# First keys and queries of the second attention in front of the last output tiles of the first, and an output bias made one product of stacked halves

## The reference, cut to what matters

```python
xn = _layernorm(x)                                   # x: 1024 x 512
s = _L0_attn_ref(xn, ...)                            # 8 heads of 8; out @ Wo_w.T + Wo_b
g = _silu(_L0_ffn_ref(xn, ...))                      # base product and 8 low-rank experts, top 2
x = x + s * g                                        # called x1 below
xn = _layernorm(x)
# second attention: 32 query heads, 8 key/value heads of 128
q = _rmsnorm((xn @ Wq.T)...); k = _rmsnorm((xn @ Wk.T)...); v = xn @ Wv.T
attn = softmax(q k / sqrt(128) + alibi, causal); s = (attn v) @ Wo.T
g = _silu(_L1_ffn_ref(xn, ...))                      # weights in 4-bit codes, two low-rank terms
x = x + s * g
```

## Time and profile before

| | us |
|---|---|
| median of three runs (lowest to highest) | 1482.02 (1481.35 to 1490.38) |
| profiled execution, its own time | 1485.61 |
| its span | 1483.8 |
| PE busy, share of the span | 1392.6 (94%) |
| DVE busy | 985.2 (66%) |
| ACT busy | 855.7 (58%) |
| POOL busy | 633.9 (43%) |
| the tail, from its first transposes (219.48) to the first matmul of slot 0 (280.16) | 60.7 |

### The profile page before, as it was taken

The page is one execution under the profiler, slowest core; times in us unless marked ns, Lnnn a source line. Parts: engine busy times, 40 slices in busy tenths (PEclk is TensorE's granted clock), DMA queues, the critical chain, the costliest instruction groups (busy, mean ns, idle before and its releaser), DMA issues.

```text
span 1483.8 us, 21377 instructions
## 1 busy us (share of the span) xinstructions
PE 1392.6 (94%) x7358; PEld 1087.5 (73%) x7358; DVE 985.2 (66%) x1851; ACT 855.7 (58%) x2103; POOL 633.9 (43%) x966
## 2 busy tenths in 40 slices
PE   4989988799999999999999999999999999989997
PEld 3733336588778888878887788888778887768786
DVE  6666644476787777777776777776786777775233
ACT  3345572465766666666766666666766666563211
POOL 4322353444454435545443445444554445433311
PEclk9989996899999999999999999999999999999999
DMA  4100021010020101011010201110020111023010
GB/s 139 64 1 1 1 94 59 15 30 30 29 73 2 58 20 54 21 39 59 15 41 19 73 20 39 42 31 30 30 72 1 44 34 38 28 66 133 15 58 28
DMA packets 35883, 61.02 MB, mean 41 GB/s; under 512 B 9056, under 2 KB 13280, under 8 KB 35776
## 3 DMA queue, kind: packets, MB, share of 16 engines
q1 hardware_dynamic: 35776, 59.66, 12.6%
HBM read 49.68 MB, written 9.96 MB: 40 GB/s over the span
## 4 chain that ended last, share of the span: by engine, by line
PE 66%; DVE 8%; issue 6%; ACT 2%; POOL 1%; DMA 0%; POOLq 0%; DVEq 0%; SPq 0%
PE T L2239 7%; PE T L1870 7%; PE T L1872 6%; PE T L1871 6%; PE S L1872 4%; PE S L1871 4%; PE S L1870 4%; PE WB L1870 4%; PE WB L1871 4%; PE WB L1872 4%; PE VB L1872 4%; PE VB L1870 4%; PE VB L1871 4%; PE T L2132 2%; DVE R L1648 2%
## 5 line engine op out<-in xcount | busy, mean ns | idle before, releaser
L848 POOL TENSOR_TENSOR RI<-SM,C 128x1 f32<-128x1 f32 x256 | 143.1, 559 | 503.7 <-ACT PB L1184 502.7
L1641 DVE CUSTOM_DVE_ANT_0 PB<-S,REL,SLC 128x128 f32<-128x128 f32 (+7 forms) x256 | 204.4, 813 | 82.3 <-PE S L1872 80.8
L1184 ACT ACTIVATE PB<-PB,NM 128x128 f32<-128x128 f32 (+7 forms) x256 | 198.9, 777 | 69.6 <-DVE NM L1641 63.5
L1249 ACT ACTIVATE R<-T 128x512 fp32r<-128x512 f32 x288 | 170.8, 594 | 100.7 <-PE T L2239 98.8
L849 POOL TENSOR_SCALAR PB<-PB,RI 128x128 f32<-128x128 f32 (+7 forms) x256 | 215.0, 840 | 25.2
L1648 DVE TENSOR_TENSOR R<-T,R 128x512 fp32r<-128x512 f32 x288 | 197.4, 688 | 42.3 <-ACT R L1249 23.8
L2239 PE MATMUL T<-C,PB 128*128 128x128 f32 x1152 | 176.6, 276 | 12.3 <-DVE R L1648 7.1
L2239 PEld LDWEIGHTS T<-C,PB 128*128 128x128 f32 x1152 | 134.1, 140 | 48.4 <-DVE R L1648 18.5
L1163 ACT ACTIVATE JUNK<-WB 128x128 bf16<-128x128 f32 x256 | 67.4, 278 | 95.2 <-PE WB L1872 95.2
L1870 PE MATMUL WB<-R,XT 128*128 128x512 f32 x288 | 117.5, 408 | 2.7 <-ACT G L1141 2.7
L1871 PE MATMUL WB<-R,XT 128*128 128x512 f32 x288 | 114.2, 397 | 0.0
(11 more groups left out here) (275 smaller groups left out, 3512.7 us busy)
## 6 DMA issues: line engine op xcount, KB each, us to landing
RAW<-w SPq DMA_DIRECT2D x86, 256.0 KB, 2.8
DQ<-codes SPq DMA_DIRECT2D x16, 352.0 KB, 3.5
DQ<-absmax SPq DMA_DIRECT2D x16, 352.0 KB, 3.0
dequantised<-DQ SPq DMA_DIRECT2D x16, 352.0 KB, 2.2
PB<-x SPq DMA_DIRECT2D x12, 256.0 KB, 3.3
PB<-dequantised SPq DMA_DIRECT2D x5, 512.0 KB, 4.4
PB<-x_scratch SPq DMA_DIRECT2D x8, 256.0 KB, 3.5
out<-PB SPq DMA_DIRECT2D x8, 256.0 KB, 2.0
```

The costliest lines, as they stand in the source:

```text
L848: ch.link(e.tensor_tensor(RI[:, k:k + 1], SM[:, k:k + 1], C[:, C_EXP + 5:C_EXP + 6], ALU.pow))
L1184: e.activation(pb(m, a, 0, L), pb(m, a, 0, L), ACT.Exp, scale=-1.0, bias=NM[:, k:k + 1], accum_out=SM[:, k:k + 1]).then_inc(exp_done, 1)
L1249: e.activation(r(PT + AT[i, ("PV", kb)] % 3 * 1024, 512), T[AT[known, it] % 2][:, :], ACT.Copy).then_inc(t_act, 1)
L1641: e.tensor_tensor_reduce(out=pb(m, a, 0, L), in0=bank[:, 0:L], in1=REL[:, TOK - L:TOK], scale=SLC[:, a:a + 1], scalar=3.0e38, op0=ALU.add, ...
```

## The change

It has three parts.

1. The tail has another order. KV 0, PQ 0 and KV 1 stand at its head, before or between the first OS and OH; KV 2, KV 3, SQ 0 and QT 0 follow in steps 1 and 2. PQ 1 now stands behind KV 6 and in front of KT 5, KT 6 and KV 7. The scores of the first query tile (new kind S0) are items of the tail and stand in front of QT 1. Keys in work lie in four buffers instead of two. `WB` goes WO 3, PQ 0, WO 4 instead of WO 3, WO 4.
2. The second, third and fourth of PQ's chunks of weights must be there earlier: their halves are made in units 27 to 31, and SP loads the last two behind the first store of x1 instead of behind four.
3. The bias product of `output0` has 64 rows of type fp32r instead of one row of float32. ACT copies the bias row on 64 partitions and makes 64 rows of 1/32 (behind the fourth of the QK products at the start of the kernel); DVE turns rows 32 to 63 into the low half in front of the first OS. The halves of O move from `OT + 512` to `PT + 1024`.

```diff
-W_AT = {("F", t): t for t in range(NT)}
+EARLY = 4
+W_AT = {}
+for _x in ([("F", t) for t in range(NT)] + [("WO", t) for t in range(EARLY)] + [("PQ", 0)] + [("WO", t) for t in range(EARLY, NT)] + [("PQ", 1)]):
+    W_AT[_x] = len(W_AT)
...
-HIGH_AT = {22: ("K", 0, 0), 23: ("K", 0, 1), 28: ("Q", 0, 0), 29: ("Q", 0, 1)}
-LOW_AT = {24: ("K", 0, 0), 25: ("K", 0, 1), 29: ("Q", 0, 0), 30: ("Q", 0, 1)}
+HIGH_AT = {22: ("K", 0, 0), 23: ("K", 0, 1), 26: ("Q", 0, 0), 27: ("Q", 0, 1), 29: ("Q", 0, 2), 30: ("Q", 0, 3)}
+LOW_AT = {24: ("K", 0, 0), 25: ("K", 0, 1), 27: ("Q", 0, 0), 28: ("Q", 0, 1), 30: ("Q", 0, 2), 31: ("Q", 0, 3)}
...
-KV_STEP = (1, 2, 3, 4, 6, 7, 8, 9)
+KV_STEP = (0, 0, 1, 2, 6, 7, 8, 10)
...
-    seq = [("XT", EARLY - 1)] if k == 0 else []
+    seq = [("XT", EARLY - 1), ("KV", 0), ("PQ", 0)] if k == 0 else []
     seq += token_items(EARLY + k, EARLY, NT)
...
+    if k == 9:
+        seq.append(("PQ", 1))
...
+    return seq + {1: [("SQ", 0)], 2: [("QT", 0)], 11: [("S0", 0), ("QT", 1)]}.get(k, [])
...
-        KN = [QN[:, 4 * HD:5 * HD], K2F[:, 3072:3200]]
+        KN = [QN[:, 4 * HD:5 * HD]] + [K2F[:, 3072 + k * P:3200 + k * P] for k in range(3)]
...
-            for t in range(EARLY):
-                store_x1(t)
+            store_x1(0)
             w1_first("Q", 0, 2)
             w1_first("Q", 0, 3)
+            for t in range(1, EARLY):
+                store_x1(t)
...
             qk(3, *QK_THEN[0])
+            act.wait_ge(in_rows, 16)
+            e.activation(r(PT + 2048, D, 64), ROWS[0:64, R_BO:R_BO + D], ACT.Copy).then_inc(bo_high, 1)
+            e.activation(r(PT + 2560, P, 64), IDENT[0:64, :], ACT.Copy, scale=0.0, bias=1.0 / 32).then_inc(ones_set, 1)
...
                     elif it[0] == "OS":
+                        if it[1] == 0:
+                            dve.wait_ge(bo_high, 1)
+                            e.tensor_tensor(R[32:64, PT + 2048:PT + 2560], ROWS[32:64, R_BO:R_BO + D],
+                                            R[32:64, PT + 2048:PT + 2560].bitcast(F32), ALU.subtract).then_inc(bo_low, 1)
...
-                e.matmul(WB[:, :], ONES, ROWS[0:1, R_BO:R_BO + D], start=True, stop=False)
+                e.matmul(WB[:, :], r(PT + 2560, P, 64), r(PT + 2048, D, 64), start=True, stop=False)
```

More of the change, by code:

```diff
@@ L260 @@
 T_LN0, T_OUT = 0, 24
-TAIL_HIGH = {0: ("Q", 0, 2), 1: ("Q", 0, 3)}
-TAIL_LOW = {1: ("Q", 0, 2), 2: ("Q", 0, 3)}
-KV_STEP = (1, 2, 3, 4, 6, 7, 8, 9)
-SC_STEP = (2, 3, 4, 5, 7, 8, 9, 10)
-KT_STEP = (3, 4, 5, 6, 8, 9, 10, 11)
-PQ_STEP, SQ_STEP, QT_STEP = (5, 9), (6, 10), (7, 11)
+KV_STEP = (0, 0, 1, 2, 6, 7, 8, 10)
+SC_STEP = (1, 1, 2, 3, 7, 8, 9, 11)
+KT_STEP = (2, 3, 4, 5, 8, 9, 10, 11)
 TAIL_STEPS = 12
 def tail_items(k):
-    seq = [("XT", EARLY - 1)] if k == 0 else []
+    seq = [("XT", EARLY - 1), ("KV", 0), ("PQ", 0)] if k == 0 else []
     seq += token_items(EARLY + k, EARLY, NT)
[L277 to L280, removed]
+    if k == 9:
+        seq.append(("PQ", 1))
+    seq += [("SC", b) for b in range(NT) if SC_STEP[b] == k]
+    if k == 11:
+        seq.append(("SQ", 1))
+    seq += [("KT", b) for b in range(NT) if KT_STEP[b] == k]
+    seq += [("KV", b) for b in range(1, NT) if KV_STEP[b] == k]
+    return seq + {1: [("SQ", 0)], 2: [("QT", 0)], 11: [("S0", 0), ("QT", 1)]}.get(k, [])
 TAIL = [x for k in range(TAIL_STEPS) for x in tail_items(k)]
@@ L543, in program @@
         ones_set = sem("ones_set")
+        bo_high = sem("bo_high")
+        bo_low = sem("bo_low")
         x1_ready = sem("x1_ready")
@@ L937, in add_x @@
             def add_x(t):
-                hold(pool, w_free, W_OUT + t + 1, p_passed)
+                hold(pool, w_free, W_AT["WO", t] + 1, p_passed)
                 hold(pool, in_x[t % 4], 16 * (t // 4 + 3), p_passed)
@@ L1127, in high_on @@
                 if t >= 2:
-                    act.wait_ge(w_full, W_OUT + t - 1)
-                e.activation(r(OT + 512 + t % 2 * 256, P), T[k % 2][:, 0:P], ACT.Copy).then_inc(high, 1)
+                    act.wait_ge(w_full, W_AT["WO", t - 2] + 1)
+                e.activation(r(PT + 1024 + t % 2 * 256, P), T[k % 2][:, 0:P], ACT.Copy).then_inc(high, 1)
             for x in range(NBX):
@@ L1209, in _ @@
                         high_q(b, T_AT[x] + 1, T[T_AT[x] % 2])
[L1210 to L1216, removed]
+                    elif kind == "S0":
+                        for a in range(4):
+                            exp1(0, a, P, a + 1)
+                    if x == ("KV", NT - 1):
+                        w1_high("K", 1, 0)
+                        w1_high("K", 1, 1)
             def lines(g, i, part):
@@ L1699, in _ @@
                     low_q(t, T_AT[x] + 1, T[T_AT[x] % 2])
-            for k in range(4):
-                dve.wait_ge(out_x1[k], 32)
-            dve.wait_ge(out_dq, 16)
+                elif kind == "S0":
+                    for k in range(4):
+                        dve.wait_ge(out_x1[k], 32)
+                    dve.wait_ge(out_dq, 16)
+                    for a in range(4):
+                        bias_max(0, a, P, S_PRO + a + 1, S[a % 2])
             dve.wait_ge(t_free, T_BASE)
             dve.sem_inc(v_split, NT)
-            for a in range(4):
-                bias_max(0, a, P, S_PRO + a + 1, S[a % 2])
             def combine(g, i, part):
@@ L2157, in _ @@
                 if kind == "PQ":
-                    project_q(block_of(b), W_PRO + b, lambda kt: C_PRO["Q", 0, kt])
+                    project_q(block_of(b), W_AT[x], lambda kt: C_PRO["Q", 0, kt])
                 elif kind == "WO":
                     output0(b, t_free, T_AT["OH", b] + 1)
+                elif kind == "S0":
+                    for a in range(4):
+                        if a < 2:
+                            pe.wait_ge(st_exp, 2 * NBX)
+                        scores1(0, a, P, a - 1 if a >= 2 else None, max(T_AT["KT", 0], T_AT["QT", 0]) + 1, S[a % 2])
                 elif kind in ("OS", "OH", "XT", "KV", "KT", "QT"):
                     k = T_AT[x]
-                    if kind in ("OS", "OH", "XT"):
+                    if kind in ("OS", "OH", "XT") or k < T_OUT + 2:
                         ring0(k)
@@ L2184, in _ @@
                         transpose_q(k, T[k % 2])
[L2185 to L2188, removed]
             def values1(g, i, kb):
```

39 lines of the change are left out of this document (16 added, 23 removed).

## The result

The changed kernel takes 1472.37 us (median of 8 executions, 1470.38 to 1474.42) against 1482.74 of the kernel before (8 executions, 1480.76 to 1490.38). The ratio on record is 0.9912, with a 95% interval of 0.9887 to 0.9937; it is estimated over all executions and is not the quotient of the two medians, which is 0.9930 and lies in the interval. By the medians that is 10.4 us or 0.7% less: within 1% of before, as forecast, and 4.1 us above the predicted 1468.3. The profiled execution took 1472.16 us, its span is 1470.4.

The account below looks back on a forecast made before the run. Bound: the last four tiles' chain from WO to XT at a low clock, and the idle end. Terms -2.2 - 5.4 - 2.3 - 4.0 + 0.2 = -13.7 us: 1485.6 to 1471.9, less 3.6: 1468.3 us; range 1460 to 1477.

Parts of the forecast that it names:

- 3.6 us: Median of the runs taken as 3.6 us below the profiled execution, so 1471.9 became 1468.3.
- The milestones: Signs behind XT 3: WO 4 ending near 13 us, XT 4 starting near 24, XT 7 ending near 35.
- The head of the tail: Start of the tail: 6.8 us of dense matmuls, so no fall of the clock 4.4 us behind XT 3.
- XT 3 to XT 4: Tail stretch: XT 4 starts at 24.0 us instead of 29.4, with a low clock between 16 and 23: -5.4 us.
- the two terms behind it: XT 4 to the end of XT 7, -2.3 us, and XT 7 to slot 0's score heads, -4.0 us.
- The bias product: The new product of 64 rows of fp32r takes 0.3 us instead of 1.05.
- The units: Units 24 to 31: four shorter products win 3.0 us, the wait for PQ's first chunk costs 0.8: -2.2 us.
- The copies: ACT's copies and DVE's subtraction for the bias, costing 0.2 us (0 to 1.0).
- XT 4 to XT 7: Stretch to the end of XT 7: 13.45 us before, now 11.2 at half clock: -2.3 us.
- the end: XT 7 to slot 0's first score heads: 23.0 us before, now 19.0: -4.0 us.
- Full clock: Rival: the clock stays full throughout the passage, sum -20.2 us, time 1461.8 us; chance 0.17.
- The dear product: Rival: the new bias product costs as much as the old, 5 us less gain, 1473.3 us; chance 0.07.

Follow-up runs that it names:

- order_only: The changed kernel with the bias product put back to one float32 row, without its two copies and subtraction: 1486.02 us, ratio 1.0003.
- bias_only: The kernel before with the third part of the change alone (bias product of 64 rows of fp32r): 1472.00 us, ratio 0.9923.
- float_64_rows: The kernel before with its float32 bias product given 64 rows instead of one: 1475.89 us, ratio 0.9951.
- fp32r_1_row: The kernel before with the new fp32r bias product cut to its first row, low half left out: 1473.05 us, ratio 0.9932.
- combined: Changed kernel, first keys' low halves before tile 7's gate, next ones after the last key's scaling, bias copies behind the router's exponential: 1471.86 us.
- after_again: The changed kernel run once more, nothing changed: 1473.55 us, ratio 0.9929 against the kernel before.
- filled: The changed kernel with 49 further matmuls that nothing reads, in front of the waits of the tail: 1468.07 us, ratio 0.9894.

## Why the prediction was right, and where it was not

**The number.** 1472.4 lies in the range, at the upper edge of the forecast's own (1464 to 1472). The sum of -13.7 answers to the profiles' -13.4, the medians' difference is 10.4. I took 3.6 us from the profiled execution as if it were a constant. It was an execution of before with a low mean clock (0.977; its executions near the median have 0.979), and the change removes low stretches, so part of the 3.6 was counted twice. The profiled execution of the changed kernel lies only 0.2 us below its median.

**The milestones** came as written or near it: WO 4's end 12.8 (12.9), XT 4 23.4 (24.0), XT 7's end 33.9 (35.2), the heads 53.8 (54 to 55), the fall of the clock 18.5 (some 15).

**The step that failed is the cause given for the clock.** "The head of the tail is now 6.8 us of dense matmuls, so I expect no fall at 4.4." The head is enough for that (order_only has it, the float32 rows, and no fall before 13.2), but it isn't needed: bias_only has no such head and no fall either. And it doesn't last: in order_only the clock falls right behind the first float32 row of the tail, and XT 4 comes at 28.8. What brings XT 4 forward is the bias product, either by its rows at an unchanged duration (float_64_rows, 7.1 us) or by its short type with one row (fp32r_1_row, 10.0). The prediction priced the product at its duration, 0.75 us each at full clock, and gave XT 3 to XT 4's 5.4 us and the two terms behind it to the order. The runs leave the order with nearly nothing (above). That the sum came out is partly luck: the order was priced too high and the product too low, and both were in the change.

**The bias product** costs 0.44 us to the next start, not 0.3. **The units** gave 1.3, not 2.2. 4 x 0.61 is 2.4; the wait for PQ's first chunk held the exponential 1.3 us, as counted (1.4), and costs 1.0 by combined, where it is gone, for my 0.8. It was the gate of tile 7 on POOL, ahead of the low halves, that made the load late.

**The copies** were put at 0.2 us. The start and units 0 to 23 lose 1.7: the first transposes of the shifts come 0.6 us later (79.57 for 78.98), which goes away in combined, and the clock is low for 20.5 us of the units instead of 17.0. after_again had 23.9, so no run ties this length to the copies.

**From XT 3 to XT 4** the working of the new order was right at full clock too (22.7 counted, 23.5 measured in filled). Its comparison was wrong: at full clock the old order takes 18.5, so the queries in front cost 5.0 us here, which the later terms return. The rows for LA were read the wrong way round: the one of 1.21 us begins 0.35 us behind the start of an addition (213.31 and 212.96 in the earlier trace rows), not ahead of it. In the changed kernel the LA of tile 4 took 0.88 us beside an addition, for the 1.0 counted.

**XT 4 to XT 7** at half clock (counted 11.2 to the end of XT 7, measured 10.5) and **the end** (19.0 counted, 20.0 measured) were right but for the scaling of the last key: 1.28 us beside POOL, 0.29 without. The Trainium skill (SBUF — State Buffer, "SBUF: two separate sides") says that DVE and GpSimd share a pair of ports as a lock, which the one that starts first holds for its whole instruction. The trace agrees: POOL starts 0.06 us ahead, and the scaling ends at 265.88, 0.1 us behind the first of POOL's two low halves (1.25 us each from 264.54).

**The rivals.** Full clock was priced at 1461.8; filled has it in the whole tail and takes 1468.1. Its three terms of the tail measured -5.9, -5.4 and -5.4 for my -6.7, -5.1 and -6.4, the units -1.3 for -2.2, and 3 us of the rest come of the 3.6 subtracted as a constant, since filled's profiled execution lies 0.8 above its median. The dear product was priced at 5 us; between float_64_rows and bias_only the duration of eight products is worth 3.9. That the old product bears on the clock stood in no rival, and its going is the largest effect of the change.

## What to carry to other kernels

When a profile shows a long low-clock stretch, look not only at idle time but at products that use few rows of the array for long; padding such a product with rows can pay without saving any work, and so can a shorter form of it with its few rows. When an order is judged by comparing a stretch with one at another clock, compare both orders at the same clock, for instance with matmuls that nothing reads. And where executions differ by their mean clock, don't subtract a profile's distance from the median as a constant.

## What the runs showed of the hardware

A float32 product of 1 row by 512 columns and one of 64 rows take PE the same 1.05 us, but with the latter the mean granted clock of the execution rises from about 0.979 to 0.986 and the kernel takes 7.1 us less (float_64_rows). With one row of fp32r, 0.44 us, it is 0.985 too (fp32r_1_row). Why the chip grants more clock for it, and whether 2 or 16 rows would do, was not tried. The long low stretch of before began with no wait of PE above 1.00 us between XT 3 and the fall. A DVE scaling of 128x128 took 0.29 us alone and 1.28 us begun just behind a POOL subtraction of 128x512. Time varied with the mean clock between executions of the same kernel by up to 16 us.
